# Feed-forward gate and up products of a hybrid block as pairs of fp32r products

## The reference

```python
def _L0_ffn_ref(x, w_gate, w_up, w_down):
    SCALE = 1.0 / 127.0                  # HIDDEN = 384, DIM = 128
    wg = _dequant(w_gate, x.dtype)       # int32 in -127..127, times SCALE
    wu = _dequant(w_up, x.dtype)
    wd = _dequant(w_down, x.dtype)
    gate = jnp.einsum('bsd,hd->bsh', x, wg)
    up = jnp.einsum('bsd,hd->bsh', x, wu)
    h = jax.nn.silu(gate) * up
    return jnp.einsum('bsh,dh->bsd', h, wd)
...
x = x + _L0_attn_a_ref(_layernorm(x, axis=-1), ...)
x = x + _L0_ffn_ref(_layernorm(x, axis=-1), ...)
x = x + _L0_attn_b_ref(_layernorm(x, axis=-1), ...)
x = x + _L0_ffn_ref(_layernorm(x, axis=-1), ...)
```

## Time and profile before

| | us |
|---|---|
| median of 3 runs (lowest to highest) | 755.37 (752.66 to 756.16) |
| the profiled execution | 755.38 |
| its span | 753.6 |
| PE busy | 611.8 (81%) |
| DVE busy | 517.9 (69%) |
| ACT busy | 390.0 (52%) |
| POOL busy | 332.1 (44%) |

### The profile page before, as it was taken

How to read it: one execution, slowest core, us unless ns; L and a number is a source line. 1 busy time by engine, 2 the same in 40 slices (tenths; PEclk the granted TensorE clock), 3 DMA queues, 4 the chain that set the end, 5 groups by cost and what they waited for, 6 DMA issues and landing times.

```text
span 753.6 us, 11260 instructions
## 1 busy us (share of the span) xinstructions
PE 611.8 (81%) x3556; PEld 364.9 (48%) x3575; DVE 517.9 (69%) x1339; ACT 390.0 (52%) x626; POOL 332.1 (44%) x295
## 2 busy tenths in 40 slices
PE   1966887888177778778999999946899699998897
PEld 1422333344022223378999888923544344544454
DVE  6679999956999799744533735387587487885052
ACT  1546667533356456356767656402266365566721
POOL 5229989800579999322678323344012012111010
PEclk9978999999589899989999999967999899999999
DMA  5700000000500000030123201522505204000001
GB/s 153 252 0 2 0 0 1 0 0 28 196 18 18 19 4 0 1 86 19 43 83 88 78 16 34 99 75 41 69 3 70 37 3 83 21 3 2 1 15 43
DMA packets 31676, 32.10 MB, mean 43 GB/s; under 512 B 5394, under 2 KB 26914, under 8 KB 31362
## 3 DMA queue, kind: packets, MB, share of 16 engines
q1 hardware_dynamic: 26274, 25.45, 14.2%
q0 software_dynamic: 2496, 5.15, 2.0%
q10 hardware_dynamic: 2848, 0.78, 0.5%
HBM read 13.90 MB, written 9.25 MB: 31 GB/s over the span
## 4 chain that ended last, share of the span: by engine, by line
PE 43%; DVE 6%; ACT 3%; issue 3%; DMA 2%; ACTq 1%; POOL 0%; DVEq 0%; POOLq 0%
PE ps L1467 40%; DVE arena L1389 3%; ACT arena L1002 2%; DMA arena<-arena 2%; PE ps L1753 1%; ACTq L994 1%; PE ps L1643 1%; DVE stats L1085 1%; DVE x L1329 1%; PE ps L1760 1%; DVE nb L1098 0%; ACT arena L991 0%; ACT arena L1010 0%; DMA arena<-moe_rows 0%; DVE mv L1088 0%
## 5 line engine op out<-in xcount | busy, mean ns | idle before, releaser
L1467 PE MATMUL ps<-arena 128*128 128x128 f32 (+12 forms) x2427 | 378.2, 341 | 69.0 <-DVE arena L1389 17.2
L1467 PEld LDWEIGHTS ps<-arena 128*128 128x128 f32 (+4 forms) x2446 | 221.9, 151 | 192.6 <-issue 77.1
L1467 PE MATMUL ps<-arena,ident 128*128 128x512 f32 x256 | 133.7, 655 | 40.4 <-DVE arena L1265 40.4
L1255 DVE TENSOR_TENSOR_SCAN arena<-ps,arena 128x512 f32<-128x512 f32 x128 | 147.5, 1202 | 8.1 <-POOL arena L769 6.0
L1389 DVE CUSTOM_DVE_ANT_0 arena<-ps,cmask 128x128 f32<-128x128 f32 (+3 forms) x256 | 115.1, 516 | 30.9 <-PE ps L1467 24.4
L769 POOL TENSOR_TENSOR arena<-arena 128x1024 f32<-128x1024 f32 x64 | 127.8, 2014 | 5.6 <-ACT arena L933 5.0
L942 ACT ACTIVATE ps<-arena 128x512 f32<-128x512 f32 x128 | 88.4, 694 | 60.1 <-DVE arena L1255 59.8
L1002 ACT ACTIVATE arena<-ps 128x1024 f32<-128x1024 f32 (+3 forms) x128 | 84.9, 709 | 58.5 <-PE ps L1467 56.3
L1467 PEld LDWEIGHTS ps<-arena,ident 128*128 128x128 f32 x256 | 50.3, 206 | 102.1 <-DVE arena L1265 56.6
L1441 DVE TENSOR_TENSOR arena<-arena,ps 128x512 f32<-128x512 f32 x46 | 31.7, 688 | 73.7 <-PE ps L1467 58.2
L754 POOL DMA_INDIRECT moe_out<-arena,xT x46 | 44.8, 974 | 73.4 <-DVE arena L1413 60.0
(11 more groups left out here) (181 smaller groups left out, 610.2 us busy)
## 6 DMA issues: line engine op xcount, KB each, us to landing
arena<-arena SPq DMA_DIRECT2D x120, 64.0 KB
moe_rows<-arena SPq DMA_DIRECT2D x2, 1495.0 KB, 11.8
arena<-moe_rows SPq DMA_DIRECT2D x8, 325.0 KB, 5.0
arena<-in_L_attn_a_Wg SPq DMA_DIRECT2D x1, 2048.0 KB, 8.5
arena<-in_L_attn_a_Wu SPq DMA_DIRECT2D x1, 2048.0 KB, 13.5
arena<-moe_out SPq DMA_DIRECT2D x4, 512.0 KB, 4.7
x<-n_L_attn_a_hidden_states SPq DMA_DIRECT2D x4, 256.0 KB, 4.9
out<-x SPq DMA_DIRECT2D x4, 256.0 KB, 2.3
```

Of the source, the lines that this page charges most:

```text
L1255: V.tensor_tensor_scan(hst[:, g % STATES, e, :], bank(6 + e), dBx[:, g % RING, e, :], 0.0, ALU.mult, ALU.add).then_inc(s_scan, 1)
L1467: return T.matmul(o, l, rr, start=start, stop=stop)
```

## The change

Gate and up are no longer one fp32 product each, but two products of type fp32r (fp32 operands rounded to fewer bits), summed in PSUM. The tokens are split in two: the high part is the transposed block rounded to fp32r by ACT's copy, the low part is what is left, subtracted by DVE (`f_low`, bank 7 minus the high part) and rounded again. [...] Both products use the same weights. `two_parts` serves all three places: the expert blocks, the ramp and the tail.

The low part lies in the memory of `r`, which is free by then; the high part lies where the tokens lay. fp32r views of the same addresses are made ahead of the tensors (`xT_rounded`, `h2T_rounded`, `xE_rounded`, `r_rounded`). `f_low` gets its own event and semaphore `s_fxl`; tiles wait for `s_fxl` in place of `s_fxT`, and so does the next user of bank 7. Its places: in the same block as `f_turn` in the expert stage; in the ramp one step (batch 2) or two half-steps (batch 3) later; in attention through `uses`; for batch 3 of pass 1 right behind `f_turn` in the tail. In `steps` the order on DVE around the first is: qk_rest(1, 0), maxima, maxima, qk(1, 1) (PE and ACT only), f_low(0, 2), combine(3), f_norm(0, 3), maxima, qk_rest(1, 1).

```diff
@@ -77,10 +77,14 @@
 
 
         x = sb("x", [P, NT, D])
+        with nc.sbuf_tensor("r_rounded", [P, NB, L], F32R) as r_rounded:
+            pass
         r = sb("r", [P, NT, D])
         NROW = D + 2
         nbr = sb("nb", [P, 2, TB, NROW])
         nb = nbr[:, :, :, 0:D]
+        with nc.sbuf_tensor("xT_rounded", [P, 2, L], F32R) as xT_rounded:
+            pass
         xT = sb("xT", [P, 2, L])
         stats = sb("stats", [P, NT, 6])
         mv = sb("mv", [P, NT, 2])
@@ -90,8 +94,8 @@
         identb = sb("identb", [P, P], BF16)
         kmask = sb("kmask", [P, P], BF16)
         neghalf = sb("neghalf", [P, NT])
-        wgT = sb("wgT", [P, HID])
-        wuT = sb("wuT", [P, HID])
+        wgT = sb("wgT", [P, HID], F32R)
+        wuT = sb("wuT", [P, HID], F32R)
         wdT = sb("wdT", [P, HT, D])
         mT = sb("mT", [P, D])
         vx = sb("vx", [P, D])
@@ -109,6 +113,12 @@
         HIDDEN_AT = 32 * 1024 - SPARE
         LATE_AT = HIDDEN_AT + 2 * HT * L
         ARENA = LATE_AT + LATE
+        H2T_AT, XE_AT = 4112, LATE_AT + 13 * L
+        with (nc.sbuf_tensor("below_h2T", [P, H2T_AT], F32),
+              nc.sbuf_tensor("h2T_rounded", [P, NB, L], F32R) as h2T_rounded,
+              nc.sbuf_tensor("below_xE", [P, XE_AT - H2T_AT - NB * L], F32),
+              nc.sbuf_tensor("xE_rounded", [P, L], F32R) as xE_rounded):
+            pass
         arena = sb("arena", [P, ARENA])
         at = [0]
 
@@ -359,6 +371,7 @@
...
+        s_fxl = sem("ffn_xT_low_part_ready")
...
@@ -404,7 +417,9 @@
 
         def ffn_input(p, b):
 
-            return (xT[:, 0, :], xT[:, 1, :], xE[:, 0:L], xT[:, 0, :])[b] if p else h2T[:, b, :]
+            high = ((xT_rounded[:, 0, :], xT_rounded[:, 1, :], xE_rounded[:, :], xT_rounded[:, 0, :])[b] if p
+                    else h2T_rounded[:, b, :])
+            return high, r_rounded[:, b, :]
 
         def o_bank(b, qt):
 
@@ -488,13 +503,13 @@
 
         PAIRS, UNITS, LAG = NH // 2, (NH // 4) * TB, 2
         HP = PAIRS // 2
-        uses = {"qk": "qk_rest", "o_turn": "o_add"}
+        uses = {"qk": "qk_rest", "o_turn": "o_add", "f_turn": "f_low"}
 
         PATTERN = (("maxima", 0, "use", "maxima", 1, "maxima", "values", "short"),
                    (0, "use", "maxima", 1, "maxima", "values", "short"))
         ramp = {(1, 1): [("combine", 2), ("f_norm", 0, 2)], (2, 0): [("f_normalise", 0, 2), ("f_turn", 0, 2)],
-                (2, 1): [("combine", 3), ("f_norm", 0, 3)], (3, 0): [("tile", 2, 0), ("f_normalise", 0, 3)],
-                (3, 1): [("tile", 2, 1), ("f_turn", 0, 3)], (4, 0): [("tile", 2, 2)], (4, 1): [("tile", 3, 0), ("f_down", 2)],
+                (2, 1): [("f_low", 0, 2), ("combine", 3), ("f_norm", 0, 3)], (3, 0): [("tile", 2, 0), ("f_normalise", 0, 3)],
+                (3, 1): [("tile", 2, 1), ("f_turn", 0, 3)], (4, 0): [("f_low", 0, 3), ("tile", 2, 2)], (4, 1): [("tile", 3, 0), ("f_down", 2)],
                 (5, 0): [("tile", 3, 1), ("f_add", 2)], (5, 1): [("tile", 3, 2), ("f_down", 3), ("f_add", 3)]}
         steps, later, use = [], [], []
         for a in range(NB * PAIRS + HP + LAG):
@@ -544,8 +559,8 @@
                   11: [("add_r", 3), ("prep", 0)], 12: [("prep", 1)], 13: [("prep", 2)], 14: [("prep", 3)],
                   15: [("prep", 4)], 16: [("prep", 5)],
                   1: [("h2turn", 0), ("targets", 0)], 22: [("targets", 1)],
-                  27: [("combine", 0), ("f_norm", 0, 0)], 28: [("f_normalise", 0, 0)], 29: [("f_turn", 0, 0)],
-                  30: [("combine", 1), ("f_norm", 0, 1)], 31: [("f_normalise", 0, 1)], 33: [("f_turn", 0, 1)],
+                  27: [("combine", 0), ("f_norm", 0, 0)], 28: [("f_normalise", 0, 0)], 29: [("f_turn", 0, 0), ("f_low", 0, 0)],
+                  30: [("combine", 1), ("f_norm", 0, 1)], 31: [("f_normalise", 0, 1)], 33: [("f_turn", 0, 1), ("f_low", 0, 1)],
                   34: [("f_down", 0)], 35: [("f_add", 0), ("norm", 0)], 36: [("normalise", 0)], 37: [("turn", 0)],
                   38: [("qk", 0, 0)], 39: [("qk_rest", 0, 0)], 40: [("qk", 0, 1)], 41: [("qk_rest", 0, 1)], 42: [("vals", 0)],
                   43: [("f_down", 1)], 44: [("f_add", 1)]}
@@ -558,10 +573,12 @@
                 items.append(("tile",) + tile_after[i])
         NITEM = len(items)
 
-        before = [("o_turn", last, 0), ("o_turn", last, 1)] + later
+        left = [part for short in later if short
+                for part in ([short, ("f_low",) + short[1:]] if short[0] == "f_turn" else [short])]
+        before = [("o_turn", last, 0), ("o_turn", last, 1)] + left
         in_ffn = {(0, 0): [("o_add", last, 0), ("o_turn", last, 2), ("o_add", last, 1)],
                    (0, 1): [("o_turn", last, 3), ("o_add", last, 2)], (0, 2): [("o_add", last, 3), ("f_norm", 1, 3)],
-                  (1, 0): [("f_normalise", 1, 3)], (1, 1): [("f_turn", 1, 3)]}
+                  (1, 0): [("f_normalise", 1, 3)], (1, 1): [("f_turn", 1, 3), ("f_low", 1, 3)]}
 
         last_ffn = before + [event for events in in_ffn.values() for event in events]
         LOAD_1, X_FROM = 15, 7
@@ -1011,7 +1028,7 @@
 
             def f_turn(p, b):
                 act.wait_ge(s_ft, p * NB + b + 1)
-                S.copy(ffn_input(p, b), bank(7)).then_inc(s_fxT, 1)
+                S.copy(ffn_input(p, b)[0], bank(7)).then_inc(s_fxT, 1)
 
             parts = dict(f_turn=f_turn, turn=turn, qk=first_part, vals=vals, place_max=place_max, scores=exps, values=outputs,
                          h2turn=lambda c: moe_input(HB + c), route=lambda: logits(1), top_a=lambda: router_exp(1), prep=prep_copies)
@@ -1373,6 +1390,11 @@
                 layernorm_end(b, b % 2, s_fn)
                 turned[0] = (s_ft, p * NB + b + 1)
 
+            def f_low(p, b):
+                dve.wait_ge(s_fxT, p * NB + b + 1)
+                high, low = ffn_input(p, b)
+                V.tensor_tensor(low, bank(7), high.bitcast(F32), ALU.subtract).then_inc(s_fxl, 1)
+
             def rest_part(b, w):
                 dve.wait_ge(s_qh, 2 * b + w + 1)
                 wait(dve, s_qp, 2 * (2 * b + w - 2) + 2)
@@ -1402,7 +1424,7 @@
                 V.tensor_tensor(yn[:, qt, :].rearrange("p (h d) -> p h d", d=HS), o[:, :, 0:HS],
                                 rs[:, qt, :].unsqueeze(2).to_broadcast([P, NH, HS]), ALU.mult).then_inc(s_yn, 1)
 
-            parts = dict(norm=norm, normalise=normalise_block, f_norm=f_norm, f_normalise=f_normalise, qk_rest=rest_part,
+            parts = dict(norm=norm, normalise=normalise_block, f_norm=f_norm, f_normalise=f_normalise, f_low=f_low, qk_rest=rest_part,
                          maxima=maxima, o_add=finish, h2norm=lambda: h2_norm(1, asked_h2), top_a=lambda: top_a(1),
                          top_b=lambda: top_b(1), slots=lambda: find_slots(1, rank_bank(1)), add_r=add_r, combine=combine,
                          targets=targets)
@@ -1755,7 +1777,7 @@
 
             def f_turn(p, b):
                 pe.wait_ge(s_fn, p * NB + b + 1)
-                bank7((s_fxT,), (p * NB + b + 1,))
+                bank7((s_fxl,), (p * NB + b + 1,))
                 for j in range(TB):
                     last = T.transpose(ps[:, 7, j * P:j * P + P], nb[:, b % 2, j, :], ident[:])
                 last.then_inc(s_ft, 1)
@@ -1767,20 +1789,26 @@
             pe.wait_ge(s_bs, 2 * CT * NS)
             block_turn(0)
             block_turn(1)
+            def two_parts(o, w, f, p, b):
+
+                high, low = ffn_input(p, b)
+                mm(o, w[:, f * P:f * P + P], high, stop=False)
+                return mm(o, w[:, f * P:f * P + P], low, start=False)
+
             def moe_tile(b, f):
                 m = item("tile", b, f)
-                pe.wait_ge(s_fxT, b + 1)
+                pe.wait_ge(s_fxl, b + 1)
                 wait(pe, s_sg, m - 1)
-                mm(bank(m % 2), wgT[:, f * P:f * P + P], ffn_input(0, b)).then_inc(s_g, 1)
+                two_parts(bank(m % 2), wgT, f, 0, b).then_inc(s_g, 1)
                 wait(pe, s_hm, m - 1)
-                mm(bank(2 + m % 2), wuT[:, f * P:f * P + P], ffn_input(0, b)).then_inc(s_u2, 1)
+                two_parts(bank(2 + m % 2), wuT, f, 0, b).then_inc(s_u2, 1)
 
             def ffn_tile(p, b, f):
                 n = tile_number(p, b, f)
-                pe.wait_ge(s_fxT, p * NB + b + 1)
+                pe.wait_ge(s_fxl, p * NB + b + 1)
                 wait(pe, s_fh, n - 1)
-                mm(bank(n % 2), wgT[:, f * P:f * P + P], ffn_input(p, b)).then_inc(s_fg, 1)
-                mm(bank(2 + n % 2), wuT[:, f * P:f * P + P], ffn_input(p, b)).then_inc(s_fu, 1)
+                two_parts(bank(n % 2), wgT, f, p, b).then_inc(s_fg, 1)
+                two_parts(bank(2 + n % 2), wuT, f, p, b).then_inc(s_fu, 1)
 
             def ffn_down(p, b):
                 q = p * NB + b
```

More of the change, by code:

```diff
@@ L144, in build @@
         selr = carve([2 * NS])
+        assert at[0] == H2T_AT
         h2T = carve([NB, L])
@@ L245, in build @@
         mrow = carve([2, L], BF16)
+        assert at[0] == XE_AT
         xE = carve([L])
```

## The result

The changed kernel takes 745.12 us (median of 4 runs, 743.66 to 749.46), the kernel before 754.93 beside it (median of 4 runs, 752.66 to 756.16). The ratio is 0.987, with a 95% interval of 0.984 to 0.990: 9.8 us faster by the medians. The profiled execution of the changed kernel took 743.66 (span 741.9), that of before 755.38, so these two traces differ by 11.7.

What follows compares the result with a forecast made beforehand. The prediction took PE to bound blocks and tail, and a PE-DVE ping-pong the ramp. Terms -4.3 (blocks), -1.7 (ramp), +1.0 (attention) and -6.7 (tail) summed to -11.7 from 755.38, giving 743.7 us, range 740.5 to 751.

Steps and rivals of the forecast that it cites:

- The price of a product: Gate and up products on PE: two fp32r records take 0.43 us a pair, against 0.86 for one fp32 product.
- the prediction's own sign: In the trace: the prediction fails if records do not step by 0.21, or the tail or ramp clock is lower.
- rival A: Gate and up products: half rate, 0.86 a pair, nothing saved and subtractions remain, 757.1 us; chance 0.13.
- The lower bound: Gate and up products: fp32r records step like bf16 ones, 0.21 apart, making 0.43 us a pair.
- B: Rival for gate and up products: fp32r at full fp32 price, 1.72 a pair, 795 us; chance 0.04.
- C: Rival for gate and up products: middle price, 0.31 a record, if weight loads don't fit under records; 748 us; chance 0.12.
- Blocks: Expert blocks: six tiles save 0.86 each, one wait before the up product of tile (0,1) loses 0.86; -4.3 us.
- Ramp: Ramp, batches 2 and 3: shorter tiles outweigh two subtractions on DVE; -1.7 us, with ends -3.3 and +0.7.
- Attention: Attention: f_low(1,0) costs its full 0.69, f_low(1,1) 0.3, f_low(1,2) nothing; +1.0 us, range 0 to 1.4.
- Tail: Tail, twelve tiles: -6.7 us, not the 10.3 of PE alone, because PE waits for DVE.
- The walk: Tail: twelve tiles followed in order through queues and releasers; at 0.43 a pair it ends at 744.26, -6.7 us.
- Rival D: Tail: PE does less, so its clock is withdrawn, matmuls double and eat the gain; 757 us or more; chance 0.05.

Runs made afterwards that it cites:

- e6: Changed kernel with each 512-column fp32r product issued as two of 256 columns, high and low in turns: 756.46 us in one run, kernel before 769.42.
- e2: Kernel before with fp32r pairs and subtraction only for batches 2 and 3 of pass 0 (ramp): 769.04 us, ratio 1.002.
- e9: Changed kernel with the three attention subtractions moved half a step later, into DVE's short slot: 759.1 us in one run, kernel before 769.42.
- e1: Kernel before with fp32r pairs and subtraction only for batches 0 and 1 of pass 0 (expert blocks): 765.2 us, ratio 0.9971.
- e11: Changed kernel with the edits of e7, e8, e9 and e10 together: 742.71 us, ratio 0.9812 to the kernel before.
- e5: Changed kernel without the low-part product, gate and up from the high part alone, subtraction kept: 757.66 us in one run, kernel before 769.42.
- e12: Changed kernel without any edit, measured again on another chip: 743.47 us, ratio 0.9838 to the kernel before.
- e10: Changed kernel with ramp tile (3,2) placed before two maxima and the add of batch 2: 743.72 us in one run, kernel before 756.02.
- e7: Changed kernel with the tail's residual add of the previous batch one tile later, behind the last hidden product: 761.72 us in one run, kernel before 769.42.
- e8: Changed kernel with combine(1), its statistics and normalise one expert block later: 747.06 us in one run, kernel before 756.02.
- e3: Kernel before with fp32r pairs and subtraction only for pass 1 (tail, with its subtractions in attention): 764.32 us, ratio 0.9961.
- e4: Kernel before with all eight subtractions and their waits added, all gate and up products still single fp32: 770.88 us, ratio 1.0034.

## Why the prediction was right, point by point

Forecast 743.7, range 740.5 to 751; measured 745.1, the profiled execution 743.66. The agreement to a tenth in the profiled one is partly luck: 0.9 of its 11.7 arose in the start, and behind it the terms miss by +0.5 (blocks), -0.4 (ramp), +0.5 (attention) and +0.2 (tail), which together leave 10.8 of the 11.7. By its own steps:

- **The price of a product.** Predicted 0.43 a pair with records 0.21 apart and 0.38 each; measured 0.46, 0.23 and 0.39 to 0.40. By its letter the prediction's own sign (it fails if the step is not 0.21) was met; but 0.23 stands next to 0.21 and far from the 0.43 of rival A. The lower bound was the right end, a few per cent too low. That an fp32r record steps like a bf16 one, and so the 0.43 in every sum, was the author's estimate, which no run of the kernel before shows; the trace of after shows 0.23 for a record of 512 columns and e6 0.12 for one of 256. The fp32 product of 0.86 is as long as four steps of 0.215, the fp32r pair of 0.46 as two of 0.23; what makes the fp32 product that long is not shown. The rivals A, B and C (0.86, 1.72, 0.62 a pair) fall with it; e6 takes away C's cause as well.
- **Blocks: -4.3 predicted, -3.75 measured.** A tile saves 0.71 (1.72 to 1.01), not 0.86: four steps make 0.92, and the first record behind other work steps by 0.32. Six make 4.3; the wait before the up product of tile (0,1) is there (0.56 of idle time, where 0.86 was counted), and 4.3 - 0.6 = 3.7. The stall stood where it was predicted; the missing half microsecond is the price of the record.
- **Ramp: -1.7 predicted, -2.09 measured** (-1.6 in e2; 2.3 to 2.9 between ramps of about the same clock, so the term was too small). qk(1,1) did wait for f_low(0,2): it starts at 510.12, 2.9 earlier than at 513.03, though everything ahead of the ramp is 4.7 earlier, so 1.8 late, as forecast (514.9 for 513.03). It is absorbed, as counted. What the prediction did not ask is what the longer wait before down(3) does to the clock (last section).
- **Attention: +1.0 predicted, +1.50 measured.** The sum of f_low(1,0) and f_low(1,1) was right (0.69 + 0.3 = 0.99 predicted, 1.09 measured) and the split was wrong: the first costs 0.45, the second 0.64. f_low(1,2) costs nothing (a3 -0.09). I had argued that 6 us of unbroken PE work cover most of f_low(1,1); e9 shows that they don't when f_low stands in the slot right behind f_turn. The other +0.5 is in a1, where e1 and e2 have 0.3 and 0.4 of it without a split pass 1. Most of it goes with a wait of PE for a DMA, 6.27 in the trace of before and 6.67 in after; e9 and e11, in which all batches are split, have 6.30 and 6.24, so the change doesn't fix its length.

Waits of PE in that stage, changed kernel (sum, count, longest):

```profile
PE ps L1489 <- DMA arena<-arena: 7.2, 2, 6.7
```

- **Tail: -6.7 predicted, -6.46 measured.** The walk gave -6.7 at 0.43 a pair and -4.9 at rival C's 0.62; an estimate on the line between them is -6.4 at 0.46. This was the largest term and the one most worked on: 8.9 us come off PE (12 x 0.80, less 0.09 in each of the 8 tiles whose first record steps by 0.32), and a good quarter of it doesn't arrive, because silu and hidden product close the loop. The order was as said: a wait before f_turn(1,3) (0.99, walk 1.4), and one before the last down projection (1.22 where it was 0.85); from one down projection to the next it takes 6.02. Wrong in detail: down(1) and down(2) wait 0.15 and 0, not 0.4 to 0.6, and down(3) waits 0.4 more than before. e5 shows the cap itself.
- **The clock.** Rival D feared it in the tail, where it stayed 1.00. The doubling it reckoned with is there in the trace of before: two fp32 records take 2.07 at a granted clock of 0.50 (513.03) and 1.02 at 1.00. In e5 it did come there. Where it cost in the changed kernel is behind the ramp, in e12 and not in the trace of after.

The terms that were off in size are the price of a product (0.46 for 0.43, which makes the half microsecond in the blocks), the ramp, too small by 0.4 or more, and the subtractions in attention, by 0.1. What no term has is the spread of executions and the lower clock behind the ramp and in attention, which costs 1.5 and 1.8 in some of them (last section). With that the median of 745.1, 1.4 above the forecast, can be understood: the profiled execution of e12, the slowest of its six at 749.59, has both. But the other three runs behind the median of 745.1 have no traces, so this is argued and not shown.

## What to carry to other kernels

Before an fp32 product is halved, follow the loop around it: here the twelve tail tiles gave 6.5 of 8.9 us, because silu on ACT (0.60) and the hidden product on DVE (0.69) close the loop and set its pace, and a further cut of 5.5 us on PE (e5) brought 1.2, which a lower clock took back. In this kernel, with the integer weights in one part (what that loses, no run measures) and at a granted clock of 1.00, two fp32r products took 0.46, or 0.55 where the first record stands behind other work, in place of 0.86 for one fp32 product, and each input took one subtraction of 0.69 on DVE. The subtraction costs something where DVE leads (0.45 in a12, 0.6 in the other slot) or where its place in DVE's queue holds others up (0.64 in a23, 0.07 in another slot). Before a wait is taken away by a new order, look for the second semaphore behind it (e10). Compare traces by stages of the program, and end a stage with an event that the edit doesn't move: a gain of 1.6 us can't be seen in whole times that spread by 5 to 9, while most stages repeat within 0.15.

## What the hardware showed that I had not expected

**The clock after a wait of 2 us.** The shorter ramp tiles leave PE waiting 1.97 to 2.22 before down(3), where it waited 1.12. In five of the eight traces with that wait the down projection ran slowly, 4.3 to 4.6 us instead of 2.9 (e5, e7, e8, e9, e12; not in after, e2, e6). In none of the six traces with a wait of 1.12 to 1.15 did it (before, e1, e3, e4, and e10 and e11, where the order was changed). Timeline of e12 and table by stretches of e12, e7 and after, round that projection:

```profile
538.62 4.44 PE L1489 MATMUL ps<-wdT,arena 128*128 128x128 f32 x24 [1.98 <-DVE arena L1443]
```

```profile
538.60:546.00 7.40, 7.10 (x43) 5.67 (x44) 2.90 (x15) 2.00 (x3) 0.00 (x0) 0.77 0.22 46
```

```profile
551.20:556.00 4.80, 4.80 (x27) 4.56 (x28) 0.28 (x1) 0.00 (x0) 0.00 (x0) 0.64 0.37 72
```

```profile
535.97:541.00 5.03, 5.01 (x40) 3.94 (x41) 2.04 (x10) 1.28 (x2) 0.00 (x0) 1.00 0.34 68
```

The same instructions behind the same wait ran at a granted clock of 0.64 to 0.77 in two executions and at 1.00 in the third. In stretches of 1 us e12 shows 0.50 from 540 to 543 and 1.00 from 544 on, e7 1.00 until 552, 0.50 from 553 to 555 and 1.00 from 556 on, so 0.77 and 0.64 are means over both. Each time it costs 1.4 to 1.6 us. So this wait of PE, some 2 us long, had a price above its length in five of eight executions. That the wait is what decides is supported by e10 and e11, but two traces aren't enough to show it.

**A second place like it.** Behind the DMA wait of 6.2 to 6.8 us in attention, the time from the first o_turn to the second is 2.89 in nine traces and 4.6 to 5.0 in e7, e8, e9, e11 and e12, which adds about 1.8 to a1. This too is the clock. The same 22 matmuls, in after and in e12, in the table by stretches:

```profile
589.66:592.55 2.89, 2.88 (x22) 1.40 (x23) 1.90 (x6) 1.52 (x2) 0.46 (x1) 1.00 0.00 0
```

```profile
593.77:598.57 4.80, 4.80 (x22) 2.27 (x23) 1.95 (x6) 1.62 (x2) 0.46 (x1) 0.58 0.00 0
```

With the 1.5 at down(3), which a1 holds too, that makes its 118.4 to 118.6 in e7, e8, e9 and e12; e5 has only the 1.5 (116.48), e11 only the 1.8 (117.37). The trace of after lacks it and that of e12, the same program, has it, so it differs between executions. But it was seen in five of the nine traces of the changed kernel and its variants (after, e5 to e12) and in none of the other five (before, e1 to e4), so whether the change makes it more frequent is open, and so is what decides it.

**Loads of 0.19, 0.12 apart.** In e6 weight loads of 0.19 start 0.12 apart, so a load's duration bounded neither the step between records there nor that between loads.
